# Normed attention of a decoder: weights centred once, the norm's weight and bias at the transposes' exit, scores on two row groups, projection two batches ahead

## What is computed

```python
k = (x @ Wk.T).reshape(b, t, h, s)
q = (x @ Wq.T).reshape(b, t, h, s)
v = (x @ Wv.T).reshape(b, t, h, s)
k = _ln(k, kln_w, kln_b)      # (k - mean) * rsqrt(var + 1e-5) * w + b, over the 16 of a head
q = _ln(q, qln_w, qln_b)
dot = jnp.einsum('bqhs,bkhs->bhqk', q, k) * scalefactor
dot = jnp.where(causal, -jnp.inf, dot)
attn = jax.nn.softmax(dot, axis=-1)
out = jnp.einsum('bhqk,bkhs->bqhs', attn, v).reshape(b, t, e)
return out @ Wu.T             # x = layernorm(x + this)
```

## Time and profile before

| | us |
|---|---|
| median of 3 runs (4431.55 to 4438.46) | 4432.09 |
| the profiled execution | 4428.92 |
| its span, first to last instruction | 4427.2 |
| changed stage, first load to the next stage's first load | 1624.6 to 2340.6 |

### The profile page before, as it was taken

The page is one execution under the profiler, slowest core; times in us unless marked ns, Lnnn a source line. Parts: engine busy times, 40 slices in busy tenths (PEclk is TensorE's granted clock), DMA queues, the critical chain, the costliest instruction groups (busy, mean ns, idle before and its releaser), DMA issues. The chain is left out here.

```text
span 4427.2 us, 82278 instructions
## 1 busy us (share of the span) xinstructions
PE 3325.3 (75%) x20398; PEld 2048.2 (46%) x20398; DVE 2349.4 (53%) x10450; ACT 2156.2 (49%) x6589; POOL 1639.2 (37%) x2356
## 2 busy tenths in 40 slices
PE   7999897889888336677775877777777776687772
PEld 5566655666666223333332444444444443444441
DVE  1222222666666755555555888888888884311112
ACT  3433342666665104444443777777777774221110
POOL 1111112555554356665652444444444442010004
PEclk9999997999999767777776778878778786799996
DMA  1000001111110010000001000000000001315673
GB/s 58 18 11 13 16 12 38 40 37 33 37 38 30 25 62 10 17 14 14 14 14 35 18 16 18 17 15 19 17 15 17 19 13 47 139 34 165 219 229 115
DMA packets 112025, 189.93 MB, mean 43 GB/s; under 512 B 11038, under 2 KB 95774, under 8 KB 105694
## 3 DMA queue, kind: packets, MB, share of 16 engines
q1 hardware_dynamic: 102238, 166.84, 12.1%
q10 hardware_dynamic: 7200, 14.68, 0.8%
q0 software_dynamic: 2400, 6.56, 0.4%
HBM read 150.43 MB, written 37.62 MB: 42 GB/s over the span
## 5 line engine op out<-in xcount | busy, mean ns | idle before, releaser
L3067 DVE MAX8 sa_cand<-sa_s 128x8 f32<-128x45 f32 (+3 forms) x3328 | 406.5, 194 | 35.8 <-ACT sa_s L2913 32.2
L672 POOL TENSOR_SCALAR ca_p<-ca_p,ca_rec 100x361 f32<-100x361 f32 x512 | 286.8, 579 | 343.8 <-DVE ca_rec L950 343.3
L2796 PE MATMUL sa_tr<-sa_ident,sa_s 128*128 128x128 f32 (+3 forms) x1248 | 282.7, 346 | 172.8 <-POOL sa_s L2672 108.3
L852 ACT ACTIVATE ca_p<-ca_sm,ca_nb 100x361 f32<-100x361 f32 x512 | 301.9, 591 | 211.0 <-DVE ca_nb L936 210.0
L2672 POOL TENSOR_SCALAR sa_s<-sa_s,sa_unit,sa_nu 128x361 f32<-128x361 f32 (+1 forms) x416 | 261.3, 644 | 308.7 <-DVE sa_nu L3158 308.7
L2796 PEld LDWEIGHTS sa_tr<-sa_ident,sa_s 128*128 128x128 f32 (+3 forms) x1248 | 189.4, 182 | 274.9 <-issue 265.0
L2921 ACT ACTIVATE sa_s<-sa_s,sa_nt 128x361 f32<-128x361 f32 (+1 forms) x416 | 243.9, 590 | 131.7 <-DVE sa_nt L3119 131.7
L1635 ACT ACTIVATE na_p<-na_sm,na_nb 100x100 f32<-100x100 f32 x512 | 187.2, 366 | 232.8 <-DVE na_nb L1714 228.3
L936 DVE CUSTOM_DVE_ANT_0 ca_sm<-ca_sc,ca_mb 100x361 f32<-100x361 f32 x512 | 252.4, 527 | 69.3 <-PE ca_sc L759 56.4
L2663 POOL TENSOR_TENSOR sa_over<-sa_cand,sa_tc 128x384 f32<-128x384 f32 (+1 forms) x128 | 113.1, 883 | 475.7 <-DVE sa_tc L3086 270.9
L2929 ACT ACTIVATE sa_spare_a<-sa_s,sa_nu 128x361 bf16<-128x361 f32 (+1 forms) x416 | 247.7, 597 | 53.5 <-DVE sa_nu L3160 53.4
(11 more groups left out here) (323 smaller groups left out, 8177.0 us busy)
## 6 DMA issues: line engine op xcount, KB each, us to landing
ea_we<-m_experts SPq DMA_DIRECT2D x40, 1024.0 KB, 6.5
ea_wd<-m_experts SPq DMA_DIRECT2D x40, 512.0 KB
ca_cTs<-cT SPq DMA_DIRECT2D x32, 361.0 KB
sa_cTs<-cT SPq DMA_DIRECT2D x32, 361.0 KB
rows_in<-me_zeros ACTq DMA_DIRECT2D x1, 7168.0 KB
ea_xe<-rows_in SPq DMA_DIRECT2D x40, 128.0 KB
rows_out<-ea_ye ACTq DMA_DIRECT2D x40, 128.0 KB
ca_ms<-mask SPq DMA_DIRECT2D x32, 141.0 KB
```

The lines of the kernel that those rows point to most:

```text
L672: ins = pool.tensor_scalar(p[:, r, j, :], p[:, r, j, :], rec[:, r, j:j + 1], 1.0, ALU.mult, ALU.mult)
L852: act.activation(p[:, r, j, :], sm[:, r % 2, j, :], ACT.Exp, bias=nb[:, r % 2, j:j + 1], scale=-1.0, accum_out=den[:, r, j:j + 1]).then_in ...
L2796: mm = pe.transpose(tr[f % 2][0:kn, c0:c0 + rows], s[0:rows, u, i, k0:k0 + kn], ident[0:rows, 0:rows])
L3067: ins = dve.max(cand[0:rows, i, q, :], s[0:rows, u, i, PART[q]:PART[q + 1]])
```

## The change

- The centring of k and q moves to the weights: once, ahead of all batches, VectorE subtracts from each group of 16 columns of the k,q weights their mean, so that every projection comes out centred. `centre` is gone; ScalarE's `squares` copies the projection out of the bank and squares it.
- The norm's weight and bias depend on the place within a head, which after the transposes is a row. `copy_kq` applies them as ScalarE's scale and bias while it copies, and multiplied by a 0/1 vector for even and odd heads it makes two versions of k (`kz`), one with the even heads and one with the odd. `affine` and `part_heads` are gone from POOL, with two broadcast loads of 256 KB.
- A head pair lies on 32 rows. A round's scores are two products on 32 rows each, two heads (200 columns) each, into two banks.
- The k,q projection of batch n+2 moves to round 1 and the v projection stands apart, for n+1 in round 3. Transposes lag the exponentials by two rounds and values by three, so that `sm`, `p` and their sums have four buffers. The output projection and the norm come two batches behind.
- One bank (`mix`) serves x, v and the output; `tr` has one bank instead of two; k and q have one.

```diff
-            pool.wait_ge(w_in, 16 * LOADS)
...
             def root(m, u):
                 n = 2 * m + u
-                stand(pool, turns, *sum2_done.at(n, 1))
-                pool.tensor_scalar(rs[:, :], total2[:, :], 1 / HD, LN_EPS, ALU.mult, ALU.add).then_inc(rs_done.sem, 1)
+                pool.wait_ge(*cn_done.at(n, 0))
+                stand(pool, turns, *sum_done.at(n, 1))
+                pool.tensor_scalar(rs[:, :], total[:, :], 1 / HD, LN_EPS, ALU.mult, ALU.add).then_inc(rs_done.sem, 1)
                 pool.wait_ge(*rs_done.at(n, 1))
                 pool.tensor_tensor(rs[:, :], rs[:, :], half[0:S, :], ALU.pow).then_inc(rs_done.sem, 1)
...
-            def affine(m, u):
...
-                pool.tensor_tensor(c[:, u, :], c[:, u, :], lw[0:S, :], ALU.mult).then_inc(ln_done.sem, 1)
-                pool.wait_ge(*ln_done.at(n, 1))
-                pool.tensor_tensor(c[:, u, :], c[:, u, :], lb[0:S, :], ALU.add).then_inc(ln_done.sem, 1)
...
-            def part_heads(m, u):
-                n = 2 * m + u
-                pool.wait_ge(*qk_done.at(n, 1))
-                for k in range(KD):
-                    pool.tensor_tensor(kd[:, u, HC * k:HC * k + HC, :], mid_bcast(kT[:, k, :], HC),
-                                       last_bcast(hm[:, :], S), ALU.mult).then_inc(kd_done.sem, 1)
...
-            def sequence(m, u, behind=True, here=True, ahead=True, beyond=True):
-                following = (m, 1) if u == 0 else (m + 1, 0)
-                if ahead:
-                    affine(*following)
-                    part_heads(*following)
-                if beyond:
-                    root(m + 1, u)
-                if behind:
-                    norm(*prev(m, u))
...
+            def sequence(m, u):
+                if there(m, u, 2):
+                    root(*shift(m, u, 2))
+                if there(m, u, -2):
+                    norm(*shift(m, u, -2))
...
+            pe.wait_ge(centred, CENTRED)
...
+            def project_kq(m, u):
                 n = 2 * m + u
                 pe.wait_ge(*xT_done.at(n, 1))
-                pe.wait_ge(*qk_done.at(n, 0))
+                pe.wait_ge(*qk_done.at(n, -1))
                 for k in range(KD):
-                    mm = pe.matmul(proj[1][0:S, :], xT[:, k * S:(k + 1) * S], wkq[:, k, :], start=(k == 0), stop=(k == KD - 1))
-                mm.then_inc(proj_done.sem, 1)
+                    mm = pe.matmul(kq[0:S, :], xT[:, u, k * S:(k + 1) * S], wkq[:, k, :], start=(k == 0), stop=(k == KD - 1))
+                mm.then_inc(kq_done.sem, 1)
...
+            def turn_kq(m, u, ahead):
+                n = 2 * m + u
+                if ahead:
+                    pe.wait_ge(*sq_done.at(n + 1, 1))
+                pe.wait_ge(*cn_done.at(n, 1))
+                for k in range(2 * KD):
+                    mm = pe.transpose(kq[:, k * S:(k + 1) * S], c[:, u, k * P:(k + 1) * P], ident[0:S, 0:S])
+                mm.then_inc(kqT_done.sem, 1)
...
+            def project_v(m, u, ahead):
+                n = 2 * m + u
+                if ahead:
+                    pe.wait_ge(*xT_done.at(n + 1, 1))
+                pe.wait_ge(*z_done.at(n, -2))
...
             def scores(m, u, r):
                 n = 2 * m + u
-                pe.wait_ge(*kd_done.at(n, r // 2 + 1))
+                if r == 0:
+                    pe.wait_ge(*qk_done.at(n, 1))
                 pe.wait_ge(*mx_done.at(n, 4 * r - 4))
-                pe.matmul(sc[r % 2][0:S, 0:4 * S], qT[:, u, r // 2, :], kd[:, u, 4 * r:4 * r + 4, :],
-                          start=True, stop=True).then_inc(sc_done.sem, 1)
+                for g in range(2):
+                    rows = slice(32 * (2 * (r % 2) + g), 32 * (2 * (r % 2) + g) + 32)
+                    pe.matmul(sc[r % 2][g][0:S, 0:2 * S], qT[rows, u, r // 2, :], kz[rows, u, r // 2, :, :],
+                              start=True, stop=True).then_inc(sc_done.sem, 1)
...
                 n = 2 * m + u
                 pe.wait_ge(*oT_done.at(n, 1))
                 pe.wait_ge(*z_done.at(n, 0))
+                if there(m, u, 4):
+                    pe.wait_ge(*xT_done.at(n + 4, 1))
+                elif there(m, u, 2):
+                    pe.wait_ge(*v_done.at(n + 2, 1))
...
+            def sequence(m, u):
+                for r in range(4):
+                    if there(m, u, (r + 1) // 4) and r < 3:
+                        scores(*lag(m, u, r, -1))
+                    if r == 2 and there(m, u, 1):
+                        turn_kq(*shift(m, u, 1), ahead=there(m, u, 2))
+                    if there(m, u, (r - 2) // 4):
+                        turn(*lag(m, u, r, 2))
+                    if there(m, u, (r - 3) // 4):
+                        values(*lag(m, u, r, 3))
+                    if r == 0 and there(m, u, 2):
+                        turn_x(*shift(m, u, 2))
+                    if r == 1 and there(m, u, 2):
+                        project_kq(*shift(m, u, 2))
+                    if r == 1 and there(m, u, -2):
+                        project_out(*shift(m, u, -2))
+                    if r == 3 and there(m, u, 1):
+                        scores(*shift(m, u, 1), 0)
+                        project_v(*shift(m, u, 1), ahead=there(m, u, 2))
...
+            def squares(m, u):
+                n = 2 * m + u
+                act.wait_ge(*kq_done.at(n, 1))
+                act.wait_ge(*sum_done.at(n, 0))
+                act.activation(c[:, u, :], kq[0:S, :], ACT.Copy)
+                act.activation(sq[:, :], kq[0:S, :], ACT.Square).then_inc(sq_done.sem, 1)
...
             def copy_kq(m, u):
                 n = 2 * m + u
-                act.wait_ge(*proj_done.at(n, 4))
-                act.wait_ge(*kd_done.at(n, 0))
-                act.activation(kT[:, :, :].rearrange("p k s -> p (k s)"), proj[1][:, 0:KD * S], ACT.Copy)
-                act.activation(qT[:, u, :, :].rearrange("p k s -> p (k s)"), proj[1][:, KD * S:2 * KD * S],
-                               ACT.Copy).then_inc(qk_done.sem, 1)
+                act.wait_ge(*kqT_done.at(n, 1))
+                for e in range(2):
+                    act.activation(kz[:, u, :, e, :], kq[:, 0:KD * S].rearrange("p (k s) -> p k s", s=S), ACT.Identity,
+                                   bias=kb[:, e:e + 1], scale=kw[:, e:e + 1])
+                act.activation(qT[:, u, :, :].rearrange("p k s -> p (k s)"), kq[:, KD * S:2 * KD * S], ACT.Identity,
+                               bias=lns[:, 3:4], scale=lns[:, 2:3]).then_inc(qk_done.sem, 1)
...
+            def sequence(m, u):
+                for r in range(4):
+                    if r == 3 and there(m, u, -1):
+                        copy_out(*shift(m, u, -1))
+                    if there(m, u, 0):
                         exps(m, u, r)
...
+                    if r == 2 and there(m, u, 1):
+                        copy_kq(*shift(m, u, 1))
+                    if r % 2 == 0 and there(m, u, (r - 2) // 4):
+                        copy_turned(*lag(m, u, r, 2))
+                    if r == 0 and there(m, u, 2):
+                        copy_x(*shift(m, u, 2))
+                    if r == 1 and there(m, u, 2):
+                        squares(*shift(m, u, 2))
+                    if r == 3 and there(m, u, 1):
+                        copy_v(*shift(m, u, 1))
...
+            columns = wkq[:, :, :].rearrange("p k n -> p (k n)")
+            dve.tensor_reduce(wsum[:, :], heads(columns), AX.X, ALU.add).then_inc(centred, 1)
+            dve.tensor_scalar(kw[:, :], par[:, :], lns[:, 0:1], None, ALU.mult).then_inc(centred, 1)
+            dve.tensor_scalar(kb[:, :], par[:, :], lns[:, 1:2], None, ALU.mult).then_inc(centred, 1)
+            dve.wait_ge(centred, 3)
+            dve.tensor_scalar(wsum[:, :], wsum[:, :], 1 / HD, None, ALU.mult).then_inc(centred, 1)
+            dve.wait_ge(centred, 4)
+            dve.tensor_tensor(heads(columns), heads(columns), last_bcast(wsum[:, :], HD), ALU.subtract).then_inc(centred, 1)
...
             def maxima(m, u, r):
                 n = 2 * m + u
-                dve.wait_ge(*exp_done.at(n, 4 * r - 4))
-                stand(dve, turns, *sc_done.at(n, r + 1))
+                dve.wait_ge(*exp_done.at(n, 4 * r - 12))
                 for j in range(4):
-                    dve.tensor_tensor_reduce(sm[:, r % 2, j, :], sc[r % 2][0:S, j * S:(j + 1) * S], cm[:, :], -1 / 4, 3e38,
-                                             ALU.add, ALU.min, nb[:, r % 2, j:j + 1]).then_inc(mx_done.sem, 1)
+                    if j % 2 == 0:
+                        stand(dve, turns, *sc_done.at(n, 2 * r + j // 2 + 1))
+                    dve.tensor_tensor_reduce(sm[:, r, j, :], sc[r % 2][j // 2][0:S, (j % 2) * S:(j % 2 + 1) * S], cm[:, :],
+                                             -1 / 4, 3e38, ALU.add, ALU.min, nb[:, r, j:j + 1]).then_inc(mx_done.sem, 1)
...
+            def sequence(m, u):
+                for r in range(4):
+                    if there(m, u, 0):
                         maxima(m, u, r)
...
```

(57 more changed lines are left out.)

254 lines of the change are left out of this document (83 added, 171 removed).

## The result

| | before | changed kernel |
|---|---|---|
| median of the runs, us | 4431.82 (4 runs) | 4316.18 (4 runs, 4311.35 to 4320.06) |
| ratio | | 0.9742, 95% interval 0.9717 to 0.9768 |
| profiled execution, us | 4428.9 | 4314.69 |

The changed kernel is 2.6% faster: 115.6 us, where the prediction promised 217. 4316 lies above the predicted 4215 and above the whole range, 4145 to 4285. The direction held, the size did not.

The account below looks back on a forecast made before the run. A ring of waits through POOL was taken to bound the kernel; afterwards a TensorE, ScalarE and VectorE ring: 12.5 + 0.33 x 5.8 = 14.4 us per batch, 28 + 25 + 31 x 14.4 = 499.4 for the stage, 4215 in all, range 4145 to 4285.

Parts of the forecast that it names:

- The ring of the earlier trace through POOL: Kernel before: k,q projection, VectorE, ScalarE, POOL's root, norm, weight and bias, then transposes, to the next k,q projection; 20.78 us.
- The row groups: Score products of 32 rows each on TensorE: taken to run side by side, 0.46 us a round, against 0.83 one after another.
- The start: From the changed stage's first load to the first maximum of batch 0: 28 us predicted, 35.0 before.
- T: Time per batch in the steady part of the changed stage, forecast 14.4 us against 21.2 before.
- the tail: From batch 31's first maximum to the next stage's first load: 25 us predicted, 24.5 before.
- the slot at the high level: One batch's time with TensorE at its high clock level throughout, along a chain of TensorE, ScalarE and VectorE: 12.5 us.
- Which level: Step choosing TensorE's clock in the new slot: 0.83, a third of the time low, from stages with a like busy share.
- The price of the low level: Extra time of a batch with TensorE wholly at its low clock level: 5.8 us, 18.3 against 12.5.
- The low sum of TensorE's work: TensorE's products and transposes of one batch added up at the low clock level: 18.1 us.
- Rival 2: TensorE's clock mostly low, one dense stretch, single banks making it wait: slot 15.7 to 18.3; 17 gives 4296; chance 0.25.
- Rival 1: TensorE's clock holds its high level: slot 12.1 to 13.3 us; 12.6 gives 4160; chance 0.20.
- the prediction's last part: Signs in the changed kernel's trace: 14 us between batches, clock 0.80 to 0.87, TensorE near 80% busy, multiplies of 0.57.

## Why the prediction was wrong

**Right.**
- The ring of the earlier trace rows through POOL bound the kernel before, as the run without the two passes shows.
- POOL leaves the path and does not hold VectorE by the power. The Trainium skill's rule (SBUF — State Buffer, "Summary: rules for kernel authors"), that a two-input VectorE operation and a GpSimd one that reads SBUF block each other fully, does not hold for this power of 100x32: 0.575 us in all 128 multiplies.
- The row groups run side by side: 0.58 against 0.84.
- The start: 27.7 against 28. The loads of 512 KB less and the five VectorE steps on the weights need no other price.
- The formula for the time, 3769 + 31 T, gives 4314 for the measured slot of 17.58; measured are 4316. Everything outside T was sized well but for the tail, 4 us longer than said (29.0 for 25).

**Wrong: T, and in it three terms.** The 98.6 us between 14.4 and 17.58 come apart so, with 13.02 as the slot at the high level.
1. "Which level. … I take 0.83, a third of the time low." This is the step that failed. (17.58 - 13.02) / 7.2 = 0.63 of a slot's worth at the low level, where 0.33 was taken; the granted clock was 0.66, not 0.83. At the prediction's own price of 5.8 that is 0.30 x 5.8 x 31 = 54 us. The figure came from other stages with a like busy share, and busy share does not tell the level: at 88% busy the changed kernel has 0.66, the one with 128-row scores 0.83 at 86%, the one with the moved projection 1.00 at 87%. The prediction had named the pause, its place ahead of the transposes and its length (2 us; measured 2.26), and had seen in the earlier trace rows that the clock falls where TensorE stops. It then averaged over stages instead of asking, in the slot itself, how much of TensorE's work runs before the clock is back.
2. The price of the low level, 18.3 - 12.5 = 5.8, was measured as 7.2: (7.2 - 5.8) x 0.63 x 31 = 27 us. The all-low slot would be 20.2 and not 18.3. That is an estimate by extension of the line: the full slot that was low longest, 18.94 us, was low for 0.82 of its time. The low sum of TensorE's work, 18.1, had two terms too small, which make it 18.7: in the changed kernel a score pair takes 0.92 to the next start (1842.42 to 1843.34) and not 0.83, and v 1.96 (1843.34 to 1845.30) and not 1.75.
3. The slot at the high level, 12.5, is 13.02: 16 us. The three copies out of the k,q bank were taken at 0.24 each, half of the 0.48 of 400 columns, and take 0.51: a plain copy of 200 columns takes 0.33, more than half of 0.48, and the scale and bias per row add 0.18 to it. That is 0.8 us per batch. The run with plain copies takes 0.54 of it away, and up to 0.40 come off its slot, so this term accounts for most of the 0.5 between 12.5 and 13.02.

**The rivals.** Rival 2 had the size: slot 17, 4296, for a range of 15.7 to 18.3. It gave two reasons. That the slot has one long dense stretch, of k,q and the output projection, fits the trace: in the slot shown the clock is back at the end of that stretch. That single banks make TensorE wait for readers does not: with the same banks and four products more the slot is 13.02. Rival 1, the clock at its high level, is what the kernel with the moved projection reaches (12.6 gives 4160 by the formula; 4158.94 measured). The change was a round away from it. Of the prediction's last part, 14 us slots, a clock of 0.80 to 0.87 and a TensorE near 80% busy failed; POOL idle ahead of each root, transposes never released by POOL, and multiplies of 0.57 held; the score pair took 0.58, a little over the 0.5 to 0.55 said.

**Open.** What exactly makes the clock fall, and what decides how soon it rises again. Filling the pause ahead of the transposes lifted it (idle products, moved projection), but two idle products did so in only 11 slots of 31, and added to the moved projection they lowered it in every second slot for a while; and the wider scores lifted it with the pause left as it was. A second bank for the turned probabilities, which might end the pause at its source, was not tried.

## What to carry to other kernels

When a change takes a wait off the critical path and TensorE becomes the fullest engine, look in the timeline for the place where it will still run dry once per iteration, and move work of its own queue there before counting on its full-speed durations; here a projection that stands one round later, with VectorE's step on its result, is worth 157 us, more than the rest of the change. Read the level from the durations of one shape at two places (0.58 and 0.99 for the same score pair) and not from the busy share, which looks best just when the clock is low. To price small operations, take a row of the same width, or split a fixed part off, and never halve a duration with its columns.

## What the runs showed of the hardware

- More TensorE work made the kernel faster: 4 idle products of 256 columns per slot took it from 4316 to 4166, and a dearer form of the scores to 4235.
- The clock settles into patterns. With two idle products all slots but the first and the last take either about 13.0 or about 17.3 us, at a clock of 1.00 or 0.70.
- In the kernel with the moved projection the first three slots are low and all later ones high, though TensorE has the same 83 instructions in the third (16.66 us) as in the fourth (12.28).
- POOL's power of 100x32 takes 5.46 us, a multiply of the same size 0.25, and the power does not hold up VectorE's two-input multiply. POOL's passes over 100x512 did: 1.58 for 0.57, and with these passes left out none of the 128 multiplies takes more than 0.58.
- ScalarE's copy of 200 columns takes 0.51 with scale and bias per row, 0.33 without.
